# ScalarE copies both heads' turned weights first, and GpSimd's attention-half work stands behind scan ends

## The reference

```python
# Mamba: a scan over time for each of 16 states
dA = exp(delta_t[..., None] * A)
h = dA * h + delta_t[..., None] * B_t[:, None, :] * u_t[..., None]
y = einsum('bdn,bn->bd', h, C_t)
...
# attention
q, k = _rope(q, k)
scores = where(causal, -inf, einsum('bhqd,bhkd->bhqk', q, k))
out = einsum('bhqk,bhkd->bhqd', softmax(scores / sqrt(DK)), v) @ wo.T + bo
```

## Time and profile before

| | us |
|---|---|
| median of 3 runs | 2493.61 (2491.66 to 2501.01) |
| the profiled execution | 2502.42, span 2500.5 |
| DVE busy | 1680.5 (67%) |
| PE busy | 2057.5 (82%) |
| ACT busy | 1187.7 (47%) |
| POOL busy | 951.3 (38%) |
| mean granted TensorE clock | 0.909 of full speed |

### The profile page before, as it was taken

One profiled execution on the slowest core, in us unless ns is written; L12 is line 12 of the kernel. 1 busy time (PEld: TensorE's weight loads), 2 busy tenths in 40 slices (PEclk: granted clock), 3 DMA queues, 4 the chain that ended last, 5 costly groups with the idle time before them and its releaser, 6 DMA issues.

```text
span 2500.5 us, 38952 instructions
## 1 busy us (share of the span) xinstructions
PE 2057.5 (82%) x11640; PEld 1430.8 (57%) x11640; DVE 1680.5 (67%) x2937; ACT 1187.7 (47%) x2702; POOL 951.3 (38%) x581
## 2 busy tenths in 40 slices
PE   4147788998899888998889878998889988989985
PEld 1013366665567556665566556665566655666764
DVE  2975678558965798558865788558876588645431
ACT  1214366345643466345653456344663456424631
POOL 0330366106920386106930277104850077203501
PEclk9558789999999999999999989998999998999997
DMA  2000002231123212231113212231123211142233
GB/s 103 0 0 17 17 35 71 91 109 43 57 70 113 69 51 74 90 110 40 61 64 119 68 42 84 67 106 56 43 68 116 85 45 55 65 133 71 71 105 116
DMA packets 82452, 175.06 MB, mean 70 GB/s; under 512 B 11448, under 2 KB 42560, under 8 KB 81984
## 3 DMA queue, kind: packets, MB, share of 16 engines
q1 hardware_dynamic: 78144, 164.05, 19.0%
q0 software_dynamic: 4096, 8.40, 1.1%
HBM read 123.71 MB, written 15.14 MB: 56 GB/s over the span
## 4 chain that ended last, share of the span: by engine, by line
PE 50%; DVE 22%; issue 14%; ACT 6%; POOL 4%; DMA 3%; SPq 1%; DVEq 0%; ACTq 0%; POOLq 0%
PE G L1065 7%; DVE HS L1542 7%; PE G L1050 5%; PE FM L1039 3%; PE FC L1027 3%; PE G L943 3%; PE G L954 3%; PE G L937 3%; ACT REG L1347 2%; DMA MW<-moe 2%; PE G L1082 2%; PE FM L907 2%; DVE maxes L1843 2%; DVE HC L1564 2%; PE FM L749 2%
## 5 line engine op out<-in xcount | busy, mean ns | idle before, releaser
L1542 DVE TENSOR_TENSOR_SCAN HS<-DA,D 128x1024 f32<-128x1024 f32 x128 | 374.8, 2928 | 20.5 <-ACT DA L1224 19.9
L1065 PEld LDWEIGHTS G<-REG 128*128 128x128 f32 x2560 | 350.4, 199 | 60.6 <-issue 50.2
L1065 PE MATMUL G<-REG 128*128 128x64 f32 x2560 | 358.6, 273 | 3.2 <-DVE REG L1855 3.2
L1967 POOL TENSOR_TENSOR Y<-Y,HC 128x1024 f32<-128x1024 f32 x114 | 269.1, 2361 | 181.3 <-DVE HC L1564 180.3
L1050 PE MATMUL G<-ident,REG 128*128 128x128 f32 x1280 | 242.1, 289 | 116.3 <-ACT REG L1347 114.0
L1347 ACT ACTIVATE REG<-G 128x128 f32<-128x128 f32 (+3 forms) x512 | 223.4, 436 | 121.4 <-PE G L1050 117.0
L1978 POOL TENSOR_TENSOR REG<-REG,cos_t 128x512 f32<-128x512 f32 x128 | 170.4, 1331 | 264.2 <-ACT REG L1323 264.1
L1050 PEld LDWEIGHTS G<-ident,REG 128*128 128x128 f32 x1280 | 149.0, 150 | 166.1 <-issue 132.6
L1339 ACT ACTIVATE REG<-G,maxes 128x128 f32<-128x128 f32 (+3 forms) x384 | 195.6, 510 | 81.9 <-DVE maxes L1843 81.9
L1981 POOL TENSOR_TENSOR REG<-REG 128x512 f32<-128x512 f32 x128 | 204.2, 1596 | 57.4 <-DMA REG<-ROT 48.8
L1039 PE MATMUL G<-REG 64*128 64x128 f32 (+3 forms) x768 | 217.8, 481 | 8.4 <-POOL REG L1981 7.4
(11 more groups left out here) (290 smaller groups left out, 4272.4 us busy)
## 6 DMA issues: line engine op xcount, KB each, us to landing
MW<-moe SPq DMA_DIRECT2D x120, 768.0 KB, 4.2
REG<-ROT SPq DMA_DIRECT2D x256, 128.0 KB
EW<-experts SPq DMA_DIRECT2D x16, 514.5 KB, 4.7
XG<-x_rows SPq DMA_DIRECT2D x8, 960.0 KB, 5.4
y_rows<-YO SPq DMA_DIRECT2D x120, 64.0 KB, 1.5
X<-xT SPq DMA_DIRECT2D x8, 256.0 KB, 6.1
W<-weights SPq DMA_DIRECT2D x1, 2048.0 KB, 9.5
REG<-xT SPq DMA_DIRECT2D x8, 256.0 KB, 3.2
```

The source lines that it names most:

```text
L1065: mm = pe.matmul(G[3][:, col:col + DK], PT[:, n % 2, c * P:(c + 1) * P], V[:, c, j * P + h * DK:j * P + (h + 1) * DK], start=c == 0, stop= ...
L1542: dve.tensor_tensor_scan(HS[:, :, :].rearrange("p h s -> p (h s)"), DA[:, n % 2, :, :].rearrange("p h s -> p (h s)"), D1[:, :, :].rearrang ...
L1967: pool.tensor_tensor(Y[:, :, :], Y[:, :, :], HC_EARLY if early else HC[:, n % 2, :, :], ALU.add).then_inc(y_add.sem, 1)
```

## The change

ScalarE: in every attention step both copies of turned weights come first, then the exponentials of the next step, each followed by its half of DA when the step has one. GpSimd: `phase_2` is written out by scan state instead of by attention step. For n = 2 to 15 it waits for the end of scan n, does gathers or scatters, adds state n-1 to Y, and then does the ropes, `add_picks` and weighing that `BEHIND_SCAN` lists for n. The last state is added at the end. The first front gets such a wait too: state n is added only behind the end of scan n+1. The `return` guest moves from step 12 to step 16, and SyncE's store of the output from behind swap 9 to behind swap 11.

```diff
-        PLACE_AT, NUMBER_AT, KEEP_AT, RETURN_STEP = 2, 9, 19, 12
-        ROWS_WITH = {EARLY: (("gather", 0), ("gather", 1)), EARLY + 1: (("gather", 2), ("gather", 3)), EARLY + 2: (("gather", 4), ("gather", 5)),
-                     EARLY + 3: (("gather", 6), ("gather", 7)), EARLY + 4: (("weigh", 0), ("add", 0)),
-                     EARLY + 5: (("scatter", 0), ("scatter", 1)), EARLY + 6: (("scatter", 2), ("scatter", 3)),
-                     EARLY + 7: (("scatter", 4), ("scatter", 5)), EARLY + 8: (("scatter", 6), ("scatter", 7))}
-        STORE_AFTER, ROWS_AFTER = 9, 13
+        PLACE_AT, NUMBER_AT, KEEP_AT, RETURN_STEP = 2, 9, 19, 16
+        BEHIND_SCAN = {2: (("gather", 0), ("gather", 1)), 3: (("gather", 2), ("gather", 3), ("rope", 2), ("rope", 3)),
+                       4: (("rope", 4), ("rope", 5)), 5: (("gather", 4), ("gather", 5), ("gather", 6), ("gather", 7)),
+                       6: (("rope", 6), ("rope", 7)), 7: (("add", 0), ("weigh", 0), ("rope", 8), ("rope", 9)),
+                       8: (("scatter", 0), ("scatter", 1), ("scatter", 2), ("scatter", 3)), 9: (("rope", 10), ("rope", 11)),
+                       10: (("scatter", 4), ("scatter", 5), ("rope", 12), ("rope", 13)), 11: (("scatter", 6), ("scatter", 7)),
+                       12: (("rope", 14), ("rope", 15))}
+        STORE_AFTER, ROWS_AFTER = 11, 13
...
                 for s in range(STEPS):
                     copy_turned(b, 2 * s)
+                    copy_turned(b, 2 * s + 1)
                     key = guest[s][0] if s in guest else (None, None)
                     if s + 1 < STEPS:
                         exponentials(b, 2 * s + 2, f)
...
-                    copy_turned(b, 2 * s + 1)
+                    if s + 1 < STEPS:
+                        exponentials(b, 2 * s + 3, f)
...
-                    if s + 1 < STEPS:
-                        exponentials(b, 2 * s + 3, f)
...
             def phase_2(b, f, t):
                 add_rotated(b, 0)
                 add_rotated(b, 1)
-                moved_rows(b, f, t, EARLY)
+                for n in range(EARLY, STATES):
+                    if f is not None:
+                        pool.wait_ge(scan_d.sem, scan_d.at(f, n + 1))
+                        pool.sem_inc(pool_passed, 1)
+                    behind_scan(b, t, n, ("gather", "scatter"))
+                    if f is not None and n > EARLY:
+                        front_step(f, n - 1)
+                    behind_scan(b, t, n, ("add", "weigh", "rope"))
                 if f is not None:
-                    front_step(f, EARLY)
-                for s in range(STEPS):
...
+                    front_step(f, STATES - 1)
                 if f is not None:
                     front_end(f)
...
                 for n in range(STATES):
+                    if n + 1 < STATES:
+                        pool.wait_ge(scan_d.sem, scan_d.at(b, n + 2))
+                        pool.sem_inc(pool_passed, 1)
                     front_step(b, n)
```

More of the change, by code:

```diff
@@ L460, in build @@
         PROJECT_AT, OUT_STEP = (2, 3), 1
-        PLACE_AT, NUMBER_AT, KEEP_AT, RETURN_STEP = 2, 9, 19, 12
-        ROWS_WITH = {EARLY: (("gather", 0), ("gather", 1)), EARLY + 1: (("gather", 2), ("gather", 3)), EARLY + 2: (("gather", 4), ("gather", 5)),
-                     EARLY + 3: (("gather", 6), ("gather", 7)), EARLY + 4: (("weigh", 0), ("add", 0)),
-                     EARLY + 5: (("scatter", 0), ("scatter", 1)), EARLY + 6: (("scatter", 2), ("scatter", 3)),
-                     EARLY + 7: (("scatter", 4), ("scatter", 5)), EARLY + 8: (("scatter", 6), ("scatter", 7))}
-        STORE_AFTER, ROWS_AFTER = 9, 13
+        PLACE_AT, NUMBER_AT, KEEP_AT, RETURN_STEP = 2, 9, 19, 16
[5 more added lines that the diff above has]
+                       12: (("rope", 14), ("rope", 15))}
+        assert EARLY == 2 and [i_ for n_ in BEHIND_SCAN for what_, i_ in BEHIND_SCAN[n_] if what_ == "rope"] == list(range(2, 2 * PAIRS))
+        STORE_AFTER, ROWS_AFTER = 11, 13
         TURN_STEPS = (24, 26, 27, 28)
@@ L2026, in phase_1, with behind_scan @@
                         front_step(f, n, True)
[L2028 to L2037, removed]
+            def behind_scan(b, t, n, kinds):
+                for what, i in BEHIND_SCAN.get(n, ()):
+                    if what not in kinds:
+                        continue
+                    if what == "rope":
+                        add_rotated(b, i)
+                    elif what == "gather" and t is not None:
                         gather(t, i)
@@ L2048, in phase_2 @@
                 add_rotated(b, 1)
-                moved_rows(b, f, t, EARLY)
-                if f is not None:
-                    front_step(f, EARLY)
-                for s in range(STEPS):
[L2053 to L2060, removed]
+                for n in range(EARLY, STATES):
[6 more added lines that the diff above has]
+                    behind_scan(b, t, n, ("add", "weigh", "rope"))
+                if f is not None:
+                    front_step(f, STATES - 1)
                 if f is not None:
```

## The result

The changed kernel takes 2560.68 us (median of 4 runs, 2557.34 to 2569.8), the kernel before 2492.64 beside it: 1.0281 of it, with a 95% interval of 1.023 to 1.0331. The prediction of 2465 and its range (2412 to 2522) are both missed, and the sign is wrong.

The account below looks back on a forecast made before the run. The prediction took no one engine to bound the whole, TensorE the last lap, and VectorE as nearly full in halves with scans. Terms -16 - 35 + 17 + 14 - 10 = -30 took 2493.6 to about 2465 us, range 2412 to 2522.

Parts of the forecast that it names:

- First front: First front: Y sums start at a scan's end, so 15 scans get shorter; -16 us, the firmest term.
- VectorE's waits in seven halves: Attention halves with scans: VectorE waits less for GpSimd, 5 us a half, counted one for one; -35 us.
- The single collisions: Attention halves: remaining VectorE waits, 1.6 and 2.2 us for conversions of steps 9 and 19; gate_weights might miss its pause.
- Start of the half: Start of each half: gathers and a Y sum delay ropes 2 and 3, scores 2.4 us later; +17 us over seven.
- ScalarE's order: Attention steps: the new order loses 7 us a half and gains 5, net 2 in seven halves; +14 us.
- it no longer holds the second copy: Some five steps where the exponential waits for late maxima: the second copy comes sooner; -5 us a half.
- Waits for rotations shrink as ScalarE comes later: Attention halves: argument against the rival that ScalarE's order decides; no size given.
- TensorE's clock: Laps 4 to 6: fewer long waits save half of the 6.4 us a lap tied to the lower clock; -10 us.
- ScalarE's order decides; slower: Rival, attention halves: ScalarE's order costs the full 7 us a half, +49; 2509 to 2528 us; chance 0.18.
- The waits only change their owner: Rival, attention halves: ropes 3, 5 and 7 become the last wait, only the front gains; 2485 us; chance 0.22.
- The pauses always let VectorE in: Rival, attention halves: VectorE gets in at every GpSimd pause, waits fall 10 us a half; 2420 us; chance 0.20.

Follow-up runs that it names:

- front_only: The kernel before with only the first front's wait for the next scan added: 2479.3 us, ratio 0.9933.
- gathers_fill: gathers_later with the C products of states 3 and 12 made eight times over as filler of TensorE's waits: 2473.41 us, ratio 0.9893.
- front_fill: front_only with the C products of states 3 and 12 made eight times over as filler of TensorE's waits: 2466.15 us, ratio 0.9909.
- gathers_later: pool_only with gathers 2 and 3 moved from behind scan 3 to behind scan 5: 2487.59 us, ratio 0.9946.
- pool_only: The changed kernel with ScalarE's old order, so GpSimd's part of the change alone: 2503.06 us, ratio 1.0028.
- plain_steps: The changed kernel with ScalarE's new order only in steps without a DA: 2514.59 us, ratio 1.006.
- da_fill: The changed kernel with the first half of DA between the two copies of turned weights, the second between the exponentials: 2492.47 us, ratio 0.9972.
- both_mends: The changed kernel with da_fill's ScalarE order and gathers 2 and 3 behind scan 5: 2490.84 us, ratio 1.0002.

## Why the prediction was wrong, by its own steps

*First front, -16:* right. -17 in front_only, by the mechanism named. Two readings on the way were off without harm: against the HC of its own state a sum starts some 3.5 later, not 1.3 (it waits for D and the next scan as well), and the earlier trace rows show no HC beside a sum; the rows of the changed kernel do (1.22 at 79.44).

*VectorE's waits in seven halves, -35:* the first half of this step was right, the second is one of the two that failed. The scans of the seven halves are 42.5 us shorter (266.4 before, 223.9 after), and the two conversions 5.2: 47.7, or 6.8 each, more than the 5 forecast. "I take it one for one, as VectorE is nearly full" is what fell. In lap 2's half it gained 7.2 (scans from 5.8 to 2.2 too much, conversions from 7.1 to 3.5), and its idle time before maxima of one bank alone grew by 13.0. At steps 22 and 23 the chain runs DA, scan, rotation, bias, copy, turn, and VectorE is one link of it. Neither gathers_fill against front_fill nor gathers_later against front_only shows any gain from it. That VectorE was busy for 119 of 134.8 was no evidence that it was the bound: time that it no longer spends inside scans and conversions turns up as idle time before maxima.

*The single collisions:* mixed. The conversion of step 9 takes 0.52, not the 1.8 forecast; that of step 19 takes 3.42, not 2.4, as it waits for a Y sum and a product. The gate did not miss its pause: its three steps in lap 2 take 0.23, 0.18 and 0.17 and are over at 887.44, and the Y sum behind the two gathers starts at 888.29.

*Start of the half, +17 (2.4 each):* right where it was read. Scan 3 starts 3.74 behind the first copy (2.95 before), and the sum of rope 3 ends 12.94 behind its start (11.27 before), so the ropes are 2.5 later in lap 2. What was not priced is what it sets off: TensorE's waits for ropes grow, and its clock is down more. gathers_later, which takes two gathers out of their way, is worth 20 us.

*ScalarE's order, +14:* the step that failed most. It measured +63 on top of GpSimd's part and +122 alone. In step 24, the one worked out, the forecast was +1.2 (by its own rows 1.5, as the copy's 0.26 was left out of the sum). The mean over laps 1 to 6 is +1.9, but that is no confirmation: with the clock up it is +0.8 (3.94 in laps 3 and 5, 3.12 before), and the rest comes with the lower clock, which takes the step to 5.85 in pool_only without the new order. So the working of one step was of the right size. But the loss was summed as independent steps and a gain of 5 a half was set against it for steps where "it no longer holds the second copy". plain_steps, which would have this gain in all steps without DA, is no faster than pool_only: 1.006 against 1.0028. The step charged other DA steps 0.5 each, about what their own work shows, and not what stands behind their second half of DA: scan, rotation, bias and copy. "Waits for rotations shrink as ScalarE comes later" was the wrong sign of that chain, since the rotation itself waits for ScalarE's DA through the scan. da_fill shows the remedy: 0.7 us of work moved into the gap of each DA step, and the cost is gone.

*TensorE's clock, -10:* wrong sign. The rows were read as if a wait of 3.12 lowered the clock and one of 2.98 didn't. The earlier trace rows have it down from 1732.70 on, 1.4 us before that wait ends, and in laps 1 and 3 it stays up at 3.13. The forecast also took fewer long waits for granted. The lower level doubled, from 126 to 253 us in the halves, and by the estimates above it explains 34 to 60 us of the 73.5. Together the terms that failed are 52 (GpSimd's part in the halves, +24 in place of -28) and 49 (ScalarE's, +63 in place of +14), and the miss is 96.

*The rivals:* "ScalarE's order decides; slower" named the right mechanism and side, but at 2509 to 2528 it bounded it with the 7 a half of single steps; the changed kernel shows 9 (63 / 7), the kernel before 17. "The waits only change their owner" describes GpSimd's part: VectorE's gain is nil, though ropes were late at the start of the half and not mainly at ropes 5 and 7. "The pauses always let VectorE in" came half true, and it did not help: where scan 8 was issued in a run of four rope instructions, it started in the 0.16 pause.

```profile
942.82 3.00 DVE L1545 TENSOR_TENSOR_SCAN HS<-DA,D 128x1024 f32<-128x1024 f32 x1
...
942.41 1.26 POOL L1981 TENSOR_TENSOR REG<-REG,cos_t 128x512 f32<-128x512 f32 x1
943.83 3.06 POOL L1984 TENSOR_TENSOR REG<-REG 128x512 f32<-128x512 f32 x1 [0.16 <-POOL REG L1981]
```

The scan took 0.7 too long and the sum behind the pause 1.8. The conversion of step 19, issued at 968.66, found no such pause: it ended at 972.08, behind a Y sum and a product that ran from 968.47 to 972.04 without one. The lock for one instruction that the Trainium skill gives (SBUF — State Buffer, "SBUF: two separate sides") agrees with the scan's row and not with the conversion's.

**Open:** how the loss in the halves splits between clock and queue beyond the estimates above, what makes the clock fall in one wait and not in an equal one, and why da_fill and both_mends still have a wait of 4.72 for the copy of step 23 in lap 2 and yet lose nothing against the kernel before. No run takes the clock's effect on a whole half away by itself.

## What to carry to other kernels

A gap in one engine's program where it waits for another is worth what is put into it: move work out of the gap, and all that stands behind comes later by that much, in every step. Before an engine's shorter waits are counted, follow the chain that ends last across engines and ask whether that engine's waits are on it; a high busy share doesn't show it. And where TensorE's clock falls in some of its waits, the work behind is slower and a later wait can be longer: compare laps of equal work first, since here they differed by 5% with nothing but the clock and the waits between them, and by 7% in pool_only.

## What the runs showed of the hardware

Adding matmuls that only write the same values again made a kernel 34 us faster (1.0281 to 1.0145); they stood ahead of TensorE's long waits, and its time at the lower level fell from 253 to 167 us. The front_fill kernel, 0.9909, and gathers_fill, 0.9893, are the fastest found here, 1% better than the kernel before. Equal laps fell into two kinds, and the length of the first long wait doesn't tell them apart: the clock was up after 2.98 and after 3.13 (laps 1 and 3), and down after 3.12 and 3.13 (lap 4). At the lower level one step of equal work, with TensorE busy throughout, took 5.85 us in place of 3.12.
